# Flow of the first layer's graph feed-forward: the slot copies are issued from GpSimd's queue instead of SyncE's

## The reference

```python
for c in range(6):
    q = ew[c, 0] * (nodes[in_q] @ We[eq] + be[eq])
    k = ew[c, 1] * (nodes[in_k] @ We[ek] + be[ek])
    v = ew[c, 2] * (nodes[in_v] @ We[ev] + be[ev])
    o = _mha(q, k, v, Wq[c], Wk[c], Wv[c], Wo[c])   # 8 heads of 16, softmax over 256 keys
    nodes[c] = act_w[c] * o + q
```

## Time and profile before

| | |
|---|---|
| median of 3 runs | 2091.3 us (2089.96 to 2099.73) |
| profiled execution | 2090.75 us |
| its span, first to last instruction | 2088.8 us |
| PE / DVE / ACT / POOL busy, whole span | 66% / 67% / 39% / 21% |
| first to last L952 (S of units 0 to 47) | 267.4 to 736.2 us |

### The profile page before, as it was taken

The page is one execution under the profiler, slowest core; times in us unless marked ns, Lnnn a source line. Parts: engine busy times, 40 slices in busy tenths (PEclk is TensorE's granted clock), DMA queues, the critical chain, the costliest instruction groups (busy, mean ns, idle before and its releaser), DMA issues. The chain is left out here.

```text
span 2088.8 us, 34728 instructions
## 1 busy us (share of the span) xinstructions
PE 1383.4 (66%) x13753; PEld 966.7 (46%) x13754; DVE 1399.1 (67%) x2126; ACT 806.9 (39%) x1151; POOL 448.6 (21%) x596
## 2 busy tenths in 40 slices
PE   0788168888888870788888833388523677140898
PEld 0565146566656640465665521266413344120797
DVE  5565446676667758577677768566586676859565
ACT  0466136666666650333333311266320477010110
POOL 6431332222222101122222200532003331000221
PEclk9999569999999995999999965599856699655798
DMA  2011322233222311000000000000000000110242
GB/s 66 3 9 10 91 64 78 79 86 79 78 78 80 90 32 62 1 1 1 1 1 1 1 11 12 12 2 2 11 0 30 1 2 2 59 20 0 86 131 94
DMA packets 97736, 76.51 MB, mean 37 GB/s; under 512 B 42612, under 2 KB 84148, under 8 KB 96692
## 3 DMA queue, kind: packets, MB, share of 16 engines
q1 hardware_dynamic: 96564, 73.10, 12.8%
q0 software_dynamic: 1024, 1.32, 0.3%
HBM read 33.10 MB, written 3.15 MB: 17 GB/s over the span
## 5 line engine op out<-in xcount | busy, mean ns | idle before, releaser
L1086 DVE TENSOR_REDUCE Mf<-bank 128x4 f32<-128x1024 f32 x192 | 234.5, 1221 | 148.6 <-PE bank L972 148.4
L1039 ACT ACTIVATE Pt<-bank 128x1024 f32<-128x1024 f32 x192 | 196.8, 1025 | 83.5 <-PE bank L990 82.8
L548 ACT ACTIVATE Pt<-bank 128x768 f32<-128x768 f32 (+1 forms) x192 | 169.4, 882 | 135.4 <-PE bank L489 134.5
L1312 POOL TENSOR_TENSOR Psum<-Pt 128x512 f32<-128x512 f32 x64 | 81.1, 1267 | 315.3 <-ACT Pt L1431 315.3
L990 PE MATMUL bank<-QK 50*128 50x256 f32 x768 | 98.9, 336 | 51.0 <-DMA QK<-NMrow 50.0
L758 PE MATMUL bank<-ident,Qf 128*128 128x128 f32 x64 | 14.3, 416 | 156.9 <-SPq L259 94.5
L1479 DVE RECIPROCAL st<-bank 128x256 f32<-128x256 f32 x64 | 111.9, 1748 | 6.9 <-PE bank L1392 6.8
L896 POOL CAST parts<-nodes 128x256 fp32r<-128x256 f32 x96 | 38.2, 397 | 339.1 <-PE bank L952 339.1
L1454 DVE TENSOR_TENSOR qk_lo<-bank,qk_hi 128x512 fp32r<-128x512 f32 x64 | 44.1, 689 | 97.1 <-ACT qk_hi L1423 97.1
L990 PEld LDWEIGHTS bank<-QK 50*128 50x128 f32 x768 | 58.8, 190 | 106.9 <-DMA QK<-NMrow 59.2
L573 DVE TENSOR_REDUCE Mx<-bank 128x2 f32<-128x256 f32 x128 | 54.3, 424 | 80.5 <-PE bank L476 76.4
(11 more groups left out here) (367 smaller groups left out, 3687.6 us busy)
## 6 DMA issues: line engine op xcount, KB each, us to landing
QK<-Z SPq DMA_DIRECT2D x288, 128.0 KB, 3.3
Wup<-in_L_upT SPq DMA_DIRECT2D x16, 512.0 KB, 3.5
Wdn<-in_L_downT SPq DMA_DIRECT2D x16, 256.0 KB, 3.7
Aup<-in_L_aupT SPq DMA_DIRECT2D x16, 128.0 KB, 3.5
QK<-NMrow SPq DMA_DIRECT2D x96, 4.0 KB
WeT<-in_L_WeT SPq DMA_DIRECT2D x1, 1280.0 KB
s_rows<-XG SPq DMA_DIRECT2D x1, 1032.0 KB, 8.2
tA<-in_x_heads SPq DMA_DIRECT2D x1, 1024.0 KB
```

What stands on the lines that cost most here:

```text
L548: act.activation(Pp[:, g % 4, :, 0:w], banks[:, 2:4, 0:w], ACT.Exp, scale=L.scale).then_inc(exp_done, 1)
L1039: act.activation(Pp[:, g % 4], banks[:, 2:4, :], ACT.Exp, scale=L.scale).then_inc(exp_done, 1)
L1086: d.tensor_reduce(m, banks[:, 0:2, :].rearrange("p h (t k) -> p h t k", t=2), AX, ALU.max).then_inc(max_done, 1)
L1312: e.tensor_tensor(Psum[:, q % 2], Pp[:, q % 4, :, 0:S], Pp[:, q % 4, :, S:2 * S], ALU.add).then_inc(key_sum, 1)
```

## The change

The branch for event D moves, unchanged, from SyncE's program to GpSimd's. SyncE keeps only N. The waits, the shapes and the semaphores are the same; the issuing engine and its position among that engine's other events differ. The page of before lists the DMAs of the two engines in different queues: SyncE's in q1, named hardware_dynamic, and those that GpSimd issues elsewhere in the kernel in q0, named software_dynamic.

```diff
-        def flow_sp(s, L, base):
+        def flow_sp(s, L):
             e = s.eng
             for kind, u, j in L.events():
                 if kind == "N":
                     ...
-                elif kind == "D":
-                    e.wait_ge(stk_done, u + 1)
-                    if u >= 3:
-                        e.wait_ge(st_full, base["P"] + L.pairs * (u - 2))
-                    for r in range(L.per):
-                        rows = slice(L.slot * r, L.slot * r + 4 * L.dh)
-                        for f, pick in enumerate((slice(1, 3), slice(1, 4, 2), slice(0, 3, 2))):
-                            o = L.slot * r + f
-                            e.dma_start(QK[o:o + 3 * L.dh:3, u % 3].bitcast(F32),
-                                        Z[rows, u % 2, pick, :].bitcast(F32)).then_inc(slots_in[u % 3], 16)
-
-        def flow_pool(g, L):
+
+        def flow_pool(g, L, base):
...
+                elif kind == "D":
+                    e.wait_ge(stk_done, u + 1)
+                    if u >= 3:
+                        e.wait_ge(st_full, base["P"] + L.pairs * (u - 2))
+                    for r in range(L.per):
+                        rows = slice(L.slot * r, L.slot * r + 4 * L.dh)
...
...
-            flow_sp(s, L0f, bases[1])
+            flow_sp(s, L0f)
...
-            flow_pool(g, L0f)
+            flow_pool(g, L0f, bases[1])
```

More of the change, by code:

```diff
@@ L898, in flow_pool @@
                         e.tensor_tensor(lo, node, hi.bitcast(F32), ALU.subtract).then_inc(parts_in, 1)
+                elif kind == "D":
[4 more added lines that the diff above has]
+                        rows = slice(L.slot * r, L.slot * r + 4 * L.dh)
+                        for f, pick in enumerate((slice(1, 3), slice(1, 4, 2), slice(0, 3, 2))):
+                            o = L.slot * r + f
+                            e.dma_start(QK[o:o + 3 * L.dh:3, u % 3].bitcast(F32),
+                                        Z[rows, u % 2, pick, :].bitcast(F32)).then_inc(slots_in[u % 3], 16)
         def flow_pe(p, L, base):
```

## The result

The changed kernel is slower, by far less than forecast: 2117.4 us (2115.1 to 2123.9, 4 runs) against 2095.5 us in the runs of before taken with it, ratio 1.011, 95% interval 1.007 to 1.015. The forecast was 2262 us, range 2140 to 2430. Its profiled execution took 2117.68 us, 26.9 us more than that of before.

A forecast was written before the change was run, and what follows sets the result against it. PE was busy 87% of the flow, otherwise mostly awaiting maxima. GpSimd's closed ring would set the pace: 3.7 + 7.26 + 2.4 + 0.1 = 13.4 us a unit, plus 10 us at node changes, +171 us: 2262 us, range 2140 to 2430.

The forecast's parts named there:

- six issues in the ring of S: On GpSimd, the next unit's parts wait for Z and six copy issues, and the PE for them: 13.4 us a unit.
- the ring: Closed loop per unit: PE's L952 to Z, six issues, next parts, back to PE; 13.4 us against 9.97.
- the issue: GpSimd's cost for six copies, 1.21 us each from the spacing of indirect gathers, 7.26 us in all.
- the lower bound: Cheapest case for GpSimd's copies: SyncE's 0.61 us each, 9.9 us a unit, +6 us.
- the two differences go against each other: Reason for 1.21 us per GpSimd copy: a gather reads indices, a copy has more pieces.
- the hand-offs: Semaphore delays between engines not in the other terms of the unit's sum, put at 0.1 us in all.
- middle: Rival: 0.65 to 0.85 us per GpSimd copy, 10.1 to 11.3 us a unit, 2107 to 2163 us; 12%.
- The node changes: In five units where weights are folded, the last B comes later: 2 us longer each, 10 us in all.
- What the change removes: SyncE's six copies ahead of the row of maxima, late in 15 of 47 units: worth 0 to 10 us, taken as 0.
- cheap issue: Rival: a GpSimd copy costs 0.6 us or less, maxima land in 1.7 us, kernel faster at 2059 us; 5%.
- The clock: PE's clock might fall in each idle gap, 1.2 us more a unit, +56 us; left out, kept in the range.
- Locked out by DVE: Rival: each GpSimd copy waits for DVE's 1.22 us reduction, up to 7.3 us a unit, 2606 us; 3%.

The follow-up runs named there:

- pool_s_first: The changed kernel with GpSimd making the next unit's parts ahead of this unit's six copies: 2102.1 us, ratio 1.0044 to the kernel before.
- quarter_ring: The changed kernel with each of the six copies cut to a quarter of its columns, same number of issues: 2120.2 us, ratio 1.013 to the kernel before.
- twelve_halves: The changed kernel with each 128 KB copy cut into two of 64 KB, twelve issues for the same bytes: 2400.8 us, ratio 1.148 to the kernel before.
- pool_s_first_gated: As pool_s_first, but the copies also wait for the second row of maxima of the unit two before: 2093.4 us, ratio 1.0001 to the kernel before.
- half_half: The changed kernel with three copies kept on GpSimd and three back on SyncE in their old place: 2095.9 us, ratio 1.0012 to the kernel before.
- both_queues: Against pool_s_first_gated, the six copies split, three each on SyncE and GpSimd at the same moment: 2055.2 us, ratio 0.981 to the kernel before.
- quarter_s_first: pool_s_first with each of the six copies cut to a quarter of its columns: 2052.5 us, ratio 0.980 to the kernel before.

## Why the prediction was wrong, point by point

**The mechanism: right.** The step "six issues in the ring of S" named the new wait (the PE at L952 for GpSimd's parts), its place and its links, and the trace shows each. pool_s_first takes the ring away and the wait goes; quarter_ring leaves it and the time stays.

**The step that failed, the term that was mis-sized: the issue,** "7.26 us in all". It measured 3.12 us from the first issue to the next cast. The forecast took the spacing of the indirect gathers as the nearest row, and kept 0.61 us, SyncE's own, only as the lower bound. The lower bound was near the truth: twelve_halves and quarter_ring show 0.6 us an issue, whatever the size. Why a gather costs twice as much was not tried; so "the two differences go against each other" was an argument with no row behind it. This one term is 4.1 us a unit, 195 us over the flow, more than the whole error of 145 us; the hand-offs, too small, and the two gaps, both below, took the rest back.

**The hand-offs were too small:** 0.1 us, where 0.49 us lie between Z and the first issue and 0.15 us between parts and PE; the parts took 2.62 us, not 2.4. With the right issue but the old hand-offs the ring would be 3.7 + 3.1 + 2.4 + 0.1 = 9.3 us, below the period of 9.7: the sum would have said "no change". Half a microsecond of hand-off decides the sign at such a margin. The rival "middle" named the measured time and, at its lower end, the ring of 10.1 us, but for an issue of 0.65 us or more. That it fits is luck: its issue is too dear by as much as its hand-offs are too short.

**The node changes: right.** Two microseconds more in five units; the issues at 397.79 and 409.91 are 12.1 us apart. In two units something was not foreseen: a gap of 2.7 us amid the six issues, with no releaser, after which the clock is low for a while, 0.50 from 501 to 506 us behind the first gap:

```profile
706.11 1.12 POOL L897 DMA_DIRECT2D QK<-Z  x2 [4.31 <-DVE Z L1097]
709.92 2.23 POOL L897 DMA_DIRECT2D QK<-Z  x4 [2.69 <-issue]
...
714.64 1.62 PE L952 MATMUL bank<-parts,wst 128*128 128x256 f32 x6 [3.55 <-POOL parts L888]
```

The sum as measured: 47 x 10.1 = 475 us, 10 for the node changes, 11 for these two gaps with what follows them (15.4, 14.8 and 11.5 us from issue to issue), 4 for slower units at the start: 500 us against 501.1. What the two gaps are stays open, but not where they stand: ahead of the 129th and the 249th of GpSimd's copies, in the changed kernel, in pool_s_first and in pool_s_first_gated alike, at different times. So they go by the count of issues, not by what the other engines do. In pool_s_first_gated the second one is this:

```profile
688.69 2.22 POOL L899 DMA_DIRECT2D QK<-Z  x4 [2.70 <-issue]
```

With 144 copies on GpSimd (half_half, both_queues) there is one gap, ahead of the 129th.

**What the change removes: half seen.** The forecast knew that B began 1.7 us after a late row and 2.4 us after a prompt one, and put the shorter time only into the rival "cheap issue". (The late row that it showed was the best case: over the 13 rows that were late, B began 1.7 to 2.7 us after the issue, 2.0 in the median.) The rival's price for an issue came true, its outcome did not. The first row did gain its 0.7 us. But copies issued right after Z are under way when the second row goes; in pool_s_first it is used 2.9 us after it is ready instead of 1.8, and a unit takes 10.07 us, all but the 10.11 of the ring. So two causes of nearly the same length lay over each other: removing the ring alone (pool_s_first) brought 13 us, removing the data alone (quarter_ring) nothing, removing both (quarter_s_first) over 60. The forecast looked at when the copies were issued, not at when their data moved.

**The clock: right as a mechanism, all but absent here.** At 10.1 us a unit the PE stands about 1 us at a time for the parts, and from 300 to 740 us the clock is 0.97, where it was 0.98. With twice the issues, the idle time that the forecast had expected came, and the clock fell with it, to 0.76.

**Locked out by DVE: no.** Six issues in 3.4 us beside a DVE at 65% leave no room for a wait of 1.2 us at each. The warning of the Trainium skill's page SBUF — State Buffer does not come to bear on the operations of this flow. It speaks of DVE in a certain mode, and no row showed that the reduction of this rival runs in it; the prediction's sum of 344 us was its own. The Trainium skill's figure of 1 us for GpSimd's path (DMA: Bandwidth & Descriptors, Specifications) is a time to the first byte; taken as an occupation it gave +115 us and was too dear also. The prediction's match of SyncE's 0.61 us an issue with the 0.6 us of that table set an issue beside a time to the first byte. Landing took 3.6 us against 3.3.

**Open.** In half_half the first row took 2.6 us although SyncE's three copies were off the DMA engines by then; only GpSimd's three, issued 0.15 us behind it, were near. In pool_s_first the same neighbours left it at 1.7 us. And the copies' data is shown as what delays the maxima by quarter_s_first and both_queues, but where in the DMA engines the row waits is not shown.

## What to carry to other kernels

Before moving work to an idle engine, write down what stands behind it in that engine's program and whether that feeds back to what the moved work waits for: a queue that was always one unit ahead becomes a ring. Put early work ahead of waiting work in the same program; here that costs two lines. For a small DMA on the critical path, look at when the big ones' data moves, half a microsecond at a time, rather than at when they are issued; here issuing a burst from two queues at once in a free stretch gained 2%, while moving it elsewhere in the unit only moved the wait.

## What the runs showed of the hardware

- In a burst GpSimd issues a plain copy of 128 KB every 0.56 us (3.38 us for six), of 64 KB every 0.60 us (7.25 us for twelve), of 32 KB every 0.58 us (3.45 us for six). SyncE's six of 128 KB take 3.87 us. An indirect gather of 41 KB costs GpSimd 0.91 us and 0.30 us behind it.
- A DMA of 4 KB is used 1.7 us after its issue with the DMA engines free, and 2.4 to 2.9 us after it when 768 KB are under way, in the same queue or the other. The one case against it is that of half_half, under "Open".
- GpSimd pauses for 2.7 us ahead of its 129th and 249th plain copy of 128 KB, whatever the other engines do at that time; with copies of 32 KB it is 1.9 us, ahead of the 114th and 216th, and with 64 KB 2.1 us, ahead of the 129th and every 108th after it.
